# Low-rank attention on one core: row and key scores in 64-row pairs, with the PSUM banks shared out anew

## The chip, the cores and the metric

One core of a Trainium2 chip runs the whole program. The metric is the device time of one execution in microseconds. The kernel before took 1809.59 us (median of three runs, 1809.46 to 1812.57). Engines are TensorE (PE, with its weight loads as PEld), VectorE (DVE), ScalarE (ACT), GpSimd (POOL) and SyncE (SP), which issues the DMAs.

## The reference

The reference is a network of five residual steps on x of 8 x 1024 x 128: a gated low-rank layer, attention in windows, the gated layer again, a quantised layer, and at last attention over low-rank projections. The change is in the last, which is cut here to what matters (8 batches, s = 1024, 8 heads, d_k = 128, d_c = d_hr = 32):

```python
c_q, c_kv = h_t @ W_DQ + b_DQ, h_t @ W_DKV + b_DKV            # 32 wide
q_c, k_c, v_c = (c_q @ W_UQ + b_UQ), (c_kv @ W_UK + b_UK), (c_kv @ W_UV + b_UV)   # split into 8 heads of 128
q_r = (c_q @ W_QR + b_QR)                                     # 8 heads of 32
k_r = h_t @ W_KR + b_KR                                       # 32, the same for all heads
scores = concat(q_c, q_r) @ concat(k_c, k_r).T / sqrt(160)
o = softmax(scores) @ v_c
x = x + o @ W_O + b_O
```

## The kernel before, in words

The program is one sequence per engine, with semaphores between them. Stages follow each other: window attention until about 500 us, the quantised layer, and from about 585 us to the end the low-rank attention, which also carries the rest of the next batch's norm and the last quantised layer ("extra items").

**The arithmetic.** The key weights are multiplied into the query weights once, so that scores are products of 64 numbers (32 of c_kv, 32 rotary) on either side. To keep precision with fp32r matmuls, both sides are split into a high and a low part. A key tensor `key_hl` holds high parts in partitions 0 to 63 and low parts in 64 to 127; `q_hi` holds the query's high part twice, `q_low` the low part and a row of shifts. A head (one of 64, numbered u) has eight steps g, each with a tile of 128 keys or query rows.

**Steps.** The code goes through steps g with an order per engine written by a planner, `low_rank_plan`. In a step PE does, for each half of 512 columns, a *row score* (line 1825, for the head whose scores come 14 steps later, `ROW_LEAD`) and the *key scores* (lines 1878 and 1882, two matmuls that accumulate). VectorE takes the maximum of each row score (line 1833) and every four steps collects them (line 1841); GpSimd makes the shifts (lines 1853, 1857) and SyncE moves them into the last row of `q_low` (line 1864), 4 DMAs for each half of a head. ScalarE takes the exponential of each half (line 1893) into `prob`, a ring of 8 tiles. GpSimd adds seven of the eight tiles of a head with six additions (lines 1904 and 1907).

At every fourth step PE weighs the values with four tiles of `prob` (line 1936), and at step 3 of 8 it also forms the totals of the head before from the added tiles and the eighth (line 1929). VectorE inverts the totals (line 1946) and multiplies (line 1953); SyncE moves the head's result away.

**Queries.** Two query items per head (line 1641, four steps apart) go to bank 7; ScalarE copies each to `q_hi` (line 1702) one step later, VectorE makes `q_low` (line 1754) a step after that, before the maxima of that step.

**Banks.** PSUM has eight banks. Key scores have a ring of three (0 to 2), the weighed values bank 3, row scores and totals a ring of three (4 to 6) and all items bank 7 (the last batch spreads some). A use of a ring waits for what emptied the bank three uses before (`row_bank_free`), an item for what emptied the item before (`low_bank_free`, line 1495).

**Extra items** are started by the planner at even steps without a query: "turn" (line 1670), "low" (line 1674, then VectorE's lines 1765 and 1768), "const" (1680), "value" (1687), "proj" (1650, then 1760), "quant" (1657) and "product" (1664, then 1743), the last two and the "quantise" steps for the layer of the batch before. Norm statistics (line 485) and aggregation (line 493) come at VectorE's steps too. Between PE and the other engines there is no other order than these semaphores, so an engine that waits holds up all that is behind it.

## Time and profile before

| | |
|---|---|
| time, median of three runs | 1809.59 us |
| the profiled execution's span | 1812.5 us |
| PE busy (weight loads) | 1670.4 us, 92% (1223.0, 67%) |
| VectorE, ScalarE, GpSimd busy | 1393.8 (77%), 1137.5 (63%), 1177.3 (65%) |
| chain that ended last | PE 54%, VectorE 11%, GpSimd 2% |
| exponentials, line 1893 | 1024 x 597 ns |
| maxima, line 1833 | 1024 x 682 ns |
| additions, lines 1904 and 1907 | 2.4 us each |

Busy times are unions over an engine's instructions. Matmuls overlap each other and the ends of their records are modelled, so on PE the distance between the starts of two matmuls says what one costs. In the chain the profile names, for each stretch, the engine whose work was waited for.

### The profile page before, as it was taken

Reading aid. Unit: us, or ns where it says so; the run is one execution under the profiler, and the core shown is the slowest. Engines: PE = TensorE matmul, PEld = TensorE weight load, DVE = VectorE, ACT = ScalarE, POOL = GpSimd, SP = SyncE. Lnnn points to the kernel's source line nnn. Section 1 sums busy time; section 2 is a strip of 40 time slices with the busy share of each in tenths; the row PEclk is TensorE's granted clock in tenths of the full one; section 3 lists DMA queues with packets and bytes.
Section 4 is the critical chain, followed back from the end, with each engine's and each line's share of the span. In section 5 each row is a group of like instructions: output and inputs, shape, how many; then the busy total and the mean of one; then the engine's idle time right before and its main releaser. Section 6 shows DMA issues by size and latency. Waiting matters only on the chain.

```text
span 1812.5 us, 39662 instructions
## 1 busy us (share of the span) xinstructions
PE 1670.4 (92%) x15057; PEld 1223.0 (67%) x15057; DVE 1393.8 (77%) x2976; ACT 1137.5 (63%) x2222; POOL 1177.3 (65%) x909
## 2 busy tenths in 40 slices
PE   4679999999877899999999999999999999999995
PEld 4557777777766567666766766766676677677674
DVE  5557777766597888878888888888887888888862
ACT  5447777777676466666666666666656666665662
POOL 4300111000066498898898988989889898898892
PEclk9889999999887899999999999999999999999997
DMA  4556666654000000000000000001001000100101
GB/s 123 136 140 156 162 156 159 164 136 116 29 1 1 1 10 8 10 8 10 7 13 16 10 8 19 11 7 22 7 10 19 8 10 7 22 7 10 19 10 30
DMA packets 198677, 81.47 MB, mean 45 GB/s; under 512 B 152553, under 2 KB 177493, under 8 KB 198357
## 3 DMA queue, kind: packets, MB, share of 16 engines
q1 hardware_dynamic: 198484, 78.93, 19.5%
q8 instruction: 119, 1.95, 0.5%
q14 instruction: 74, 0.60, 0.1%
HBM read 39.79 MB, written 29.88 MB: 38 GB/s over the span
## 4 chain that ended last, share of the span: by engine, by line
PE 54%; DVE 11%; POOL 2%; issue 1%; ACT 1%; DMA 0%; SPq 0%; POOLq 0%; ACTq 0%
PE pair L1825 12%; PE pair L1878 11%; PE pair L1882 11%; PE pair L1936 10%; DVE amax L1833 4%; PE pair L1929 4%; PE pair L1650 2%; DVE o_inv L1946 1%; PE pair L1641 1%; DVE stats L485 1%; POOL w_mix L1907 1%; PE pair L1664 1%; DVE q_low L1754 1%; DVE cq L1765 1%; DVE key_hl L1768 1%
## 5 line engine op out<-in xcount | busy, mean ns | idle before, releaser
L1893 ACT ACTIVATE prob<-pair 128x512 f32<-128x512 f32 x1024 | 604.4, 597 | 422.2 <-PE pair L1882 359.6
L1833 DVE TENSOR_REDUCE amax<-pair 128x1 f32<-128x512 f32 x1024 | 670.3, 682 | 133.9 <-PE pair L1825 131.8
L1825 PE MATMUL pair<-key_hl,q_hi 128*128 128x512 f32 x1024 | 437.8, 430 | 11.2 <-DVE amax L1833 7.1
L1878 PE MATMUL pair<-q_hi,key_hl 128*128 128x512 f32 x1024 | 405.2, 396 | 2.6 <-ACT prob L1893 2.6
L1882 PE MATMUL pair<-q_low,key_h 65*128 65x512 f32 x1024 | 406.0, 396 | 0.0
L1907 POOL TENSOR_TENSOR w_mix<-w_mix,prob 128x1024 f32<-128x1024 f32 x160 | 382.3, 2389 | 25.2 <-ACT prob L1893 8.5
L1907 POOL TENSOR_TENSOR Wm<-Wm,prob 128x1024 f32<-128x1024 f32 x155 | 369.6, 2384 | 20.8 <-ACT prob L1893 4.1
L520 POOL TENSOR_SCALAR veps<-mv 128x8 f32<-128x8 f32 x47 | 11.4, 243 | 452.6 <-DVE mv L493 451.2
L1825 PEld LDWEIGHTS pair<-key_hl,q_hi 128*128 128x128 f32 x1024 | 196.1, 192 | 115.9 <-issue 51.0
L1936 PE MATMUL pair<-prob,values 128*32 128x256 f32 x4096 | 247.2, 382 | 0.0
L1186 DVE TENSOR_REDUCE mx_neg<-pair 128x4 f32<-128x512 f32 x256 | 164.9, 687 | 94.8 <-PE pair L1090 94.1
L1878 PEld LDWEIGHTS pair<-q_hi,key_hl 128*128 128x128 f32 x1024 | 195.5, 191 | 44.3 <-ACT prob L1893 9.4
L1882 PEld LDWEIGHTS pair<-q_low,key_h 65*128 65x128 f32 x1024 | 192.5, 188 | 44.6
L1936 PEld LDWEIGHTS pair<-prob,values 128*32 128x32 f32 x4096 | 127.5, 110 | 100.9 <-issue 25.0
L1136 ACT ACTIVATE yT<-pair 128x512 f32<-128x512 f32 x256 | 138.6, 593 | 72.3 <-PE pair L1042 70.3
L1946 DVE RECIPROCAL o_inv<-pair 128x256 f32<-128x256 f32 x64 | 112.5, 1758 | 59.8 <-PE pair L1929 59.8
L542 ACT ACTIVATE y<-x,mean_neg,rstd 128x128 f32<-128x128 f32 x336 | 137.7, 485 | 19.0 <-POOL mean_neg L528 18.9
L1090 PE MATMUL pair<-keys,queries 64*128 64x128 f32 x1024 | 100.5, 317 | 0.0
L1042 PE MATMUL pair<-queries,keys 64*128 64x128 f32 x1024 | 97.0, 309 | 0.0
L1702 ACT ACTIVATE q_hi<-pair 128x512 fp32r<-128x512 f32 x128 | 75.7, 591 | 20.0 <-PE pair L1641 20.0
L1754 DVE TENSOR_TENSOR q_low<-pair,q_hi 64x512 fp32r<-64x512 f32 x128 | 86.3, 675 | 2.2 <-ACT q_hi L1702 2.2
L1090 PEld LDWEIGHTS pair<-keys,queries 64*128 64x128 f32 x1024 | 82.7, 199 | 3.7
(209 smaller groups left out, 2232.8 us busy)
## 6 DMA issues: line engine op xcount, KB each, us to landing
rows_mem<-once SPq DMA_DIRECT2D x128, 128.0 KB, 2.0
queries<-rows_mem SPq DMA_DIRECT2D x64, 256.0 KB, 4.5
keys<-rows_mem SPq DMA_DIRECT2D x16, 1024.0 KB, 7.1
rows_mem<-once SPq DMA_DIRECT2D x128, 64.0 KB, 1.9
q_low<-shift_cols SPq DMA_DIRECT2D x512, 0.5 KB, 2.0
yT<-o_norm SPq DMA_DIRECT2D x256, 32.0 KB, 1.9
x<-x_dram SPq DMA_DIRECT2D x8, 512.0 KB, 7.3
out_dram<-x SPq DMA_DIRECT2D x7, 512.0 KB, 3.4
```

The costliest lines, as they stand in the source:

```text
L542: ins = e.activation(y_of(stage, b)[:, t, :], x[:, b * NT + t, :], ACT.Identity, bias=mean_neg[:, k, t:t + 1], scale=rstd[:, k, t:t + 1])
L1090: ins = e.matmul(bank(S_BANKS[r])[:, q * P:(q + 1) * P], queries[rows, hb % QUERY_BUFS, q, m].rearrange("p s w -> p (s w)"), keys[rows, b ...
L1136: e.activation(pT[:, u % P_TURNED].rearrange("p q k -> p (q k)"), key_row_bank(*divmod(u, 2)), ACT.Exp).then_inc(*exps.up(u))
L1186: e.tensor_reduce(mx_neg[:, hb % 2, r, :, m], bank(S_BANKS[r]).rearrange("p (q k) -> p q k", q=QUADS), AX_X, ALU.max, negate=True).then_in ...
L1825: e.matmul(row_bank(("row", r, i)), q_hi[:, k, t * P:(t + 1) * P], key_hl[:, b % 2, i * HALF:(i + 1) * HALF], start=True, stop=True, skip_ ...
L1833: e.tensor_reduce(amax1[:, u % 2, t, i:i + 1], row_bank(("row", r, i)), AX_X, ALU.max).then_inc(*row_maxed.up((r, i)))
L1878: e.matmul(bank(j), key_hl[:, b % 2, ks], q_hi[:, k, sl], start=True, stop=False, skip_group_check=True)
L1882: e.matmul(bank(j), key_h1[:, b % 2, ks], q_low[:, k, sl], start=False, stop=True, skip_group_check=True).then_inc(*key_scored.up((g, half)))
L1893: e.activation(prob1[:, g % P_BUFS, half * HALF:(half + 1) * HALF], bank(K_BANKS[(2 * g + half) % 3]), ACT.Exp, scale=SCALE1).then_inc(*ke ...
L1907: e.tensor_tensor(into, into, p, ALU.add).then_inc(*summed_keys.up(g))
L1936: ins = e.matmul(bank(PVB)[q * DC:(q + 1) * DC, 0:QUARTER], values[:, b % 2, t, :], prob1[:, g % P_BUFS, q * QUARTER:(q + 1) * QUARTER], s ...
L1946: e.reciprocal(o_inv[:, u % 2, :], row_bank(("total", u, 0))[:, 0:QUARTER]).then_inc(*o_inverse.up(u))
```

## The change

All of it is in the low-rank stage (and a few names beside it):

- **Row scores.** Keys are kept as `key_high` and `key_low`, each with the same 64 rows in partitions 0 to 63 and 64 to 127. Queries are kept as 128 x 512: the first 512 queries in the upper 64 partitions, the last 512 in the lower. A row step issues two matmuls of 64 rows, one for each side, on 128 queries of either side and 512 keys. Row scores use the high parts alone. Both sides' banks are waited for ahead of the first.
- **Key scores.** Four matmuls of 64 rows for each side of a tile (high x high, low x high, high x low, ones x shift), in two banks; a ring of two pairs of banks (0 to 3). Key scores come ahead of row scores in a step.
- **Exponentials.** One of 128 x 1024 over both banks of a tile.
- **Query.** One item per head, at step 7 of 8, two matmuls that accumulate in one bank; `q_low` is one operation of 128 x 512.
- **Banks.** Weighed values in bank 4; banks 5, 6, 7 are one ring for rows, queries, items and totals.
- **Items** start at step 3 of 8 only, up to two: one ahead of the totals (not "low") and one behind the weighing. Projections move from step 12 to 18 of a batch's 64, the quantise steps by 4.
- **Totals.** Five additions instead of six; the totals are formed from three parts. They are inverted straight from PSUM as before: the functions of another way (`spread_out`) stand in the code but `spread_out` is always False.
- **Shift.** One maximum over the head's eight tiles, one pair of shift operations, eight DMAs into a tensor of its own, `q_shift`.
- "low" has three operations on VectorE instead of two, "value" sixteen matmuls instead of eight.

```diff
-PIPELINE = 16
+PIPELINE = 17
+PVB, SHARED_BANKS = 4, (5, 6, 7)
+SUMMED = 6
...
+    def use(key):
+        places[key] = SHARED_BANKS[len(uses) % 3], uses[-3] if len(uses) >= 3 else None
+        uses.append(key)
+        return places[key]
...
+        u, rest = divmod(g + PIPELINE, NT)
+        return ("query", u, 0) if rest == 0 and 0 <= u < U else None
...
+        if 0 <= g + ROW_LEAD < NT * U:
+            for side in range(2):
+                use(("row", g + ROW_LEAD, side))
         item = regular(g)
-        if item is None and waiting and (g % 2 == 0 or g >= NT * U):
+        if item is None and waiting and (g >= NT * U or g % NT == 3 and waiting[0][0] != "low"):
             item = waiting.pop(0)
...
+        if g % NT == 3 and 0 <= g // NT - 1 < U:
+            use(("total", g // NT - 1, 0))
+        if g % NT == 3 and 0 <= g < NT * U and waiting and (item is None or waiting[0][0] != "low"):
+            run = begin(waiting.pop(0))
+            after.append((tuple(run[:3]), 1))
...
+        def pe_row_scores(e, r):
+
+            u, t, half = row_tiles(r)
             b, k = u // NH, u % Q_BUFS
-            e.wait_ge(*q_hi_done.at((u, t // 4)))
+            e.wait_ge(*q_hi_done.at((u, 0)))
...
+            for side in range(2):
+                shared_bank_free(e, ("row", r, side))
+            for side in range(2):
+                rows = slice(side * KR, (side + 1) * KR)
+                e.matmul(shared_bank(("row", r, side)), q_hi[rows, k, t * P:(t + 1) * P],
+                         key_high[rows, b % 2, half * HALF:(half + 1) * HALF], start=True, stop=True,
+                         skip_group_check=True).then_inc(*row_scored.up((r, side)))
...
+            if g >= 2:
+                e.wait_ge(*key_exp.at(g - 2))
+            for part in range(4):
...
+                for side in range(2):
+                    rows = slice(side * KR, (side + 1) * KR)
+                    weights = ones_shift[rows, :] if part == 3 else (key_low if part == 1 else key_high)[rows, b % 2, ks]
+                    moving = (q_hi, q_hi, q_low, q_shift)[part][rows, k, :]
+                    ins = e.matmul(banks[side], weights, moving, start=part == 0, stop=part == 3, skip_group_check=True)
...
+            e.activation(prob1[:, g % P_BUFS, :], pair[g % 2][:, :], ACT.Exp, scale=SCALE1).then_inc(*key_exp.up(g))
...
-                    e.wait_ge(*summed_keys.at(NT * u + 6))
-                    parts = prob1[:, (NT * u + 7) % P_BUFS, :], key_sum[u % 2]
+                    e.wait_ge(*summed_keys.at(NT * u + SUMMED - 1))
+                    parts = *(prob1[:, (NT * u + t) % P_BUFS, :] for t in range(SUMMED, NT)), key_sum[u % 2]
...
-                for half in range(2):
-                    if 0 <= g + ROW_LEAD < total:
-                        pe_row_scores(e, g + ROW_LEAD, half)
-                    if 0 <= g < total:
-                        pe_key_scores(e, g, half)
+                if 0 <= g < total:
+                    pe_key_scores(e, g)
+                if 0 <= g + ROW_LEAD < total:
+                    pe_row_scores(e, g + ROW_LEAD)
```

## Rows read from the trace of the kernel before

**Rows 1.** The page's part 1: busy time, share, instructions.

```profile
PE 1670.4 (92%) x15057; PEld 1223.0 (67%) x15057; DVE 1393.8 (77%) x2976; ACT 1137.5 (63%) x2222; POOL 1177.3 (65%) x909
```

**Rows 2.** Line 1946's inversions: all, and two eight heads apart (timeline: start, duration).

```profile
L1946 DVE RECIPROCAL o_inv<-pair x64: 1757/1758/1759, 635.5 to 1783.7; 128x256 f32<-128x256 f32 x64
...
775.76 1.76 DVE L1946 RECIPROCAL o_inv<-pair 128x256 f32<-128x256 f32 x1 [0.80 <-PE pair L1929]
...
924.53 1.76 DVE L1946 RECIPROCAL o_inv<-pair 128x256 f32<-128x256 f32 x1 [0.80 <-PE pair L1929]
```

**Rows 3.** Groups: count, busy us, mean ns, idle before and its releaser.

```profile
L1893 ACT ACTIVATE prob<-pair 128x512 f32<-128x512 f32 x1024 | 604.4, 597 | 422.2 <-PE pair L1882 359.6
...
L1254 ACT ACTIVATE d_q<-yT,cst 128x1024 fp8e4<-128x1024 f32 x7 | 8.0, 1141 | 0.0
...
L1254 ACT ACTIVATE d_q<-yT,cst 128x512 fp8e4<-128x512 f32 x2 | 1.4, 722 | 1.7 <-POOL yT L1247 1.7
```

**Rows 4.** Timeline of VectorE in a head without extra items.

```profile
690.73 1.76 DVE L1946 RECIPROCAL o_inv<-pair 128x256 f32<-128x256 f32 x1 [0.43 <-PE pair L1929]
...
707.37 1.76 DVE L1946 RECIPROCAL o_inv<-pair 128x256 f32<-128x256 f32 x1 [0.43 <-PE pair L1929]
```

**Rows 5.** Timeline of PE in the same head.

```profile
692.89 0.39 PE L1882 MATMUL pair<-q_low,key_h 65*128 65x512 f32 x1
693.12 0.40 PE L1825 MATMUL pair<-key_hl,q_hi 128*128 128x512 f32 x1
...
698.02 0.40 PE L1882 MATMUL pair<-q_low,key_h 65*128 65x512 f32 x1
698.35 1.93 PE L1936 MATMUL pair<-prob,values 128*32 128x256 f32 x32
700.22 0.50 PE L1825 MATMUL pair<-key_hl,q_hi 128*128 128x512 f32 x1
...
706.24 0.64 PE L1929 MATMUL pair<-prob,ones_col 128*32 128x256 f32 x8
706.69 0.61 PE L1929 MATMUL pair<-w_mix,ones_col 128*32 128x256 f32 x8
```

**Rows 6.** Timeline, all engines, around a start and around a release.

```profile
1040.61 0.39 PE L1825 MATMUL pair<-key_hl,q_hi 128*128 128x512 f32 x1
...
1041.04 0.69 DVE L1833 TENSOR_REDUCE amax<-pair 128x1 f32<-128x512 f32 x1 [0.24 <-PE pair L1825]
...
1051.65 0.63 DVE L493 BATCH_NORM_AGGREGATE mv<-stats 128x2 f32<-128x6 f32 x8
...
1052.78 1.27 DVE L1833 TENSOR_REDUCE amax<-pair 128x1 f32<-128x512 f32 x2
...
1053.51 0.19 PEld L1825 LDWEIGHTS pair<-key_hl,q_hi 128*128 128x128 f32 x1 [0.90 <-DVE amax L1833]
...
1053.84 0.39 PE L1878 MATMUL pair<-q_hi,key_hl 128*128 128x512 f32 x1
```

**Rows 7.** Timeline of PE in the window stage: matmuls of 64 rows in pairs.

```profile
401.31 0.39 PE L1085 MATMUL pair<-mask_bf,both_rows 64*128 64x512 bf16 x2 [0.17 <-DVE mx_neg L1186]
401.35 0.74 PE L1090 MATMUL pair<-keys,queries 64*128 64x128 f32 x8
401.93 0.39 PE L1035 MATMUL pair<-both_rows,mask_bf 64*128 64x512 bf16 x2
```

**Rows 8.** Timelines: shift DMAs, statistics, a projection, one operation of a low product.

```profile
833.40 1.24 SPq L1864 DMA_DIRECT2D q_low<-shift_cols  x2
...
1046.30 0.86 DVE L485 BATCH_NORM_STATS2 stats<-x 128x6 f32<-128x128 f32 x4
...
781.89 1.95 PE L1650 MATMUL pair<-w_out,yT 128*128 128x128 f32 x16
783.60 0.48 PE L1825 MATMUL pair<-key_hl,q_hi 128*128 128x512 f32 x1
...
827.42 0.75 DVE L1765 SCALAR_TENSOR_TENSOR cq<-pair,Wt,cq 32x512 fp32r<-32x512 f32 x1
```

More of the change, by code:

```diff
@@ L251, in regular @@
     def regular(g):
-        for i in range(2):
-            u, rest = divmod(g + 16 - 4 * i, NT)
-            if rest == 0 and 0 <= u < U:
-                return "query", u, i
-        return None
-    opening = {"bias": [((("bias", 0, 0), None, None), 1)]}
+        u, rest = divmod(g + PIPELINE, NT)
+        return ("query", u, 0) if rest == 0 and 0 <= u < U else None
+    opening, had = {"bias": [((("bias", 0, 0), None, None), 1)]}, {}
     for item, j in zip(prepare(0), (2, 3, 4, 5, 2, 3)):
-        run = begin(item, j)
-        opening.setdefault(item[0], []).extend((tuple(run[:3]), part) for part in range(1, PARTS[item[0]] + 1))
+        opening.setdefault(item[0], []).extend(((item, j, had.get(j)), part) for part in range(1, PARTS[item[0]] + 1))
+        had[j] = item
     steps, running, waiting = [], [], []
@@ L1636, in pe_low_part @@
                 return
-            low_bank_free(e, before)
+            if item not in places_m or before:
+                low_bank_free(e, before)
             if kind == "query":
@@ L1683, in pe_low_part @@
             else:
-                e.wait_ge(*mla_built.at("both"))
+                e.wait_ge(*mla_built.at("first dims"))
                 e.wait_ge(*keys_done.at((a, 1)))
+                e.wait_ge(*key_copied.at((a, 1)))
                 for t in range(NT):
-                    ins = e.matmul(bank(j)[:, t * DC:(t + 1) * DC], key_hl[:, a % 2, t * P:(t + 1) * P], both_parts[:, :],
-                                   start=True, stop=True, skip_group_check=True)
+                    for part in (key_high, key_low):
+                        ins = e.matmul(bank(j)[:, t * DC:(t + 1) * DC], part[:, a % 2, t * P:(t + 1) * P],
+                                       first_dims[:, :], start=part is key_high, stop=part is key_low,
+                                       skip_group_check=True)
                 ins.then_inc(*value_done.up(a))
@@ new lines, in pool_shift @@
+        def pool_shift(e, u):
+            b, h = divmod(u, NH)
+            top, mc = (shift[:, n, :] for n in range(2))
+            c = ccol[:, b % 2, :, h]
+            e.wait_ge(*row_topped.at(u))
+            e.wait_ge(*const_ready.at(b))
+            if u:
+                e.wait_ge(*shift_steps.at((u - 1, 2)))
+            e.tensor_tensor(mc, top, c, ALU.add).then_inc(*shift_steps.up((u, 1)))
+            e.wait_ge(*shift_steps.at((u, 1)))
+            if u:
+                e.wait_ge(*shift_ready(u - 1))
+            e.tensor_tensor(shift_cols[:, :], c, mc, ALU.subtract).then_inc(*shift_steps.up((u, 2)))
@@ new lines, in sync_move_shift @@
+        def sync_move_shift(e, u):
+            e.wait_ge(*shift_steps.at((u, 2)))
+            queries_free(e, u)
+            if u == 0:
+                e.wait_ge(*set_low.at("shift rows"))
+            for t in range(NT):
+                side, n = divmod(t, NT // 2)
+                e.dma_start(q_shift[side * KR:side * KR + 1, u % Q_BUFS, n * P:(n + 1) * P].bitcast(F32).rearrange(
+                    "o (p t) -> o p t", t=1), shift_cols[:, t:t + 1].bitcast(F32)).then_inc(
+                    shift_moved[u % Q_BUFS], 16)
@@ L1822, in pe_row_scores, with pe_key_scores @@
+        def pe_key_scores(e, g):
+            u, t = divmod(g, NT)
+            b, k = u // NH, u % Q_BUFS
+            ks = slice(t * P, (t + 1) * P)
+            banks = [bank(g % 2 * 2 + side) for side in range(2)]
             if u % NH == t == 0:
                 e.wait_ge(*keys_done.at((b, 1)))
-            row_bank_free(e, ("row", r, i))
-            e.matmul(row_bank(("row", r, i)), q_hi[:, k, t * P:(t + 1) * P], key_hl[:, b % 2, i * HALF:(i + 1) * HALF],
-                     start=True, stop=True, skip_group_check=True).then_inc(*row_scored.up((r, i)))
@@ L1896, in pool_sum @@
+        def act_exponentials(e, g):
+            if g >= P_BUFS:
+                before = g - P_BUFS
+                e.wait_ge(*pv_done.at(before // 4))
+                if before % NT < SUMMED:
+                    e.wait_ge(*summed_keys.at(max(before % NT, 1) + before // NT * NT))
+            for side in range(2):
+                e.wait_ge(*key_scored.at((g, side)))
+            e.activation(prob1[:, g % P_BUFS, :], pair[g % 2][:, :], ACT.Exp, scale=SCALE1).then_inc(*key_exp.up(g))
         def pool_sum(e, g):
@@ L2013, in pe_low_rank @@
                     pe_weigh(e, g // 4 - 1)
+                for (item, j, before), part in after:
+                    pe_low_part(e, item, j, before, part)
         def act_low_rank(e):
-            for g, early, late in plan_m:
+            for g, early, late, after in plan_m:
                 if g == LAST_C["copy"]:
@@ L2056, in dve_low_rank @@
         def dve_low_rank(e):
-            for g, early, late in plan_m:
+            for g, early, late, after in plan_m:
                 if g == CONST_AT + 1:
```

300 lines of the change are left out of this document (157 added, 143 removed).

## The prediction, before the result was known

> **What bounds the kernel now.** I read the page first. TensorE is busy 92% of the span and no other engine over 77% [rows 1]; but the ends of its records are modelled, so I went on to the views by time. The changed part runs from about 585 us to the end, 64 heads one after another. Eight heads take 924.53 - 775.76 = 148.8 us [rows 2], 18.6 us each, and all others the same but for the first and last eight; the list of groups gives durations [rows 3]; the timelines of PE and VectorE over one head show what binds.
>
> A head with nothing but its own work takes 707.37 - 690.73 = 16.64 us between two inversions [rows 4]. On PE the starts of 512-column matmuls are 0.234 us apart (692.89 to 693.12; 0.234 as a mean over many), also where the rows differ (128 or 65): one slot [rows 5]. Going from scores to weighing adds 0.10 (698.02 to 698.35). One part of the totals, and likewise one tile weighed, costs 0.44 (706.24 to 706.69, less the 0.01 of a first group); four are 1.76, and from 698.35 to 700.22 and the 0.10 of a bare load (below) are 1.97, so coming back costs 0.2. PE needs 50 slots x 0.234 = 11.7, weighing 3.5, totals 0.9, changes 0.6: 16.7 us. **PE is exactly the bound of a clean head**. The other 148.8 - 8 x 16.64 = 15.7 us of a batch are extra PE items (about 11: projections, turns, low-rank products) and some 4 of stalls.
>
> Those stalls are the key. The row scores go to PSUM banks that VectorE must empty by a maximum. A maximum begins 0.43 us after its matmul starts (1040.61 to 1041.04), lasts 0.69, and frees the bank; the next weight load starts 0.05 after that end (first of the two at 1052.78, mean 0.68, ends 1053.46; load 1053.51), and the load itself then lies bare: next start after 0.335 instead of 0.234, so 0.10 more [rows 6]. **Chain matmul, maximum, bank free, matmul: 0.43 + 0.69 + 0.15 = 1.28 us.** Before, a half row uses the bank of three half rows earlier, 3 x 0.70 = 2.10 us: slack 0.82. At 1053.5 VectorE had come from 1.13 us of other work (1051.65 to 1052.78), and PE, full before, idled there: the slack is what is used up first [rows 6].
>
> **The change part by part.**
>
> *Row scores in 64-row pairs*: 8 pair slots a head instead of 16, if the two sides run together. The window stage shows such pairs: two 512-column matmuls of 64 rows end within 0.39 us, the time of one, and 2 x 512 + 8 x 128 columns take 401.93 - 401.31 = 0.62 us [rows 7], where one after another they would need 4 x 0.234 = 0.94. So a pair costs one slot, and I take 0.234. Gain 8 x 0.234 = 1.87. *Key scores*: four pair slots a tile instead of four: nothing. *Query*: two matmuls as before. *Totals* from three parts instead of two: +0.44. Changes of mode: +0.1 (64 to 128 rows before the query). PE work of a clean head: 40 slots 9.4, query 0.47, weighing 3.5, totals 1.3, changes 0.7: **15.35 us**, 1.3 below before.
>
> *Banks.* Three banks now carry both sides of every row step, the query, the totals and every extra item. Row step g+1 takes the banks of (g-1, side 1) and (g, side 0): it must wait for the first maximum of the step right before it. A step of PE is 5 slots = 1.17, the chain is 1.28: slack is -0.11 where it was +0.82. And step 1 of each head takes the bank of the query, which is free only when VectorE has written q_low, queued behind both maxima of step 0. Going by the durations above (VectorE starts the next maximum 0.60 after the last when both are ready: 1.27 for two [rows 6]), with R for the start of a row step, R0 = 0:
> step 0 maxima 0.43 and 1.03; q_low 1.63 to 2.30; R1 = 2.45 (PE alone: 1.17). Maxima 2.88, 3.48; R2 = 3.73. Small maximum 4.20; maxima 4.28, 4.88; R3 = 5.11. The totals take the bank of (2, side 1): 5.56 + 0.15 = 5.71. Totals to 7.0, weighing to 8.75, change 0.19, four slots: R4 = 9.87. Then three chains: R5 = 11.14, R6 = 12.42, R7 = 13.70. The query takes the bank of (6, side 1): 14.30; two slots, change, weighing, change, four slots: R0' = **17.7 us**. That is 1.07 more than 16.64 though PE works 1.3 less; PE idles 2.4.
>
> *Extra work in a batch* (the plan puts items only at step 3 of 8, one before the totals and one behind the weighing): projections 16 x 0.107 twice (781.89 to 783.60) [rows 8] = 3.8 with changes; by the same 0.11 a matmul turns 8, const and value 24, transposes 8, products 16, with 0.1 to 0.3 for each change or bank: 1.2, 2.9, 1.2, 2.0. The two low products are dear: 0.9 + 0.1 on PE (fp32, taken as twice the 0.47 of two slots; 0.47 is the lower bound), and then VectorE does three operations of 0.75 at step 5 instead of two, 2.3 in a row [rows 8], ahead of the row maxima, while row step 5 waits for their bank: +2.8 each, together 7.6. Statistics (0.86 with its end, 0.8) and aggregation (0.63) at steps 1 and 2 [rows 6, 8], twice a batch, and one reduction of 0.6 lie bare in the chain: 3.5. At steps 0 and 4 the weighing hides them. Sum 22.2. A full batch: 8 x 17.7 + 22.2 = 163.8, against 148.8: **+15.0**.
>
> *Exponentials of 128x1024*: 0.60 for 512 columns, and line 1254 takes 0.42 more for 1024 than for 512 columns (1.141, 0.722): 1.02; above that 1.14 (all of line 1254) and 1.19 (two of 0.60) [rows 3]. Key step g+2 needs exponential g: 0.43 + 1.02 + 0.15 = 1.60 from its last matmul, and comes after 1.28 + 0.47 = 1.75. At 1.14 it still fits, at 1.19 it would cost 0.02 a step. Nothing. *Five additions*: GpSimd loses one of six a head; with 65% [rows 1] it isn't the bound, so nothing; only in the last two heads, where no row scores are left, may its chain count: 0 to -5, taken as -3. *Shift*: one group of eight DMAs behind one maximum instead of two of four; issues are 0.6 apart [rows 8], so 5 us, and a few to land, ready near 12 of the 16.8 us there are, under the row and key scores between. Cover 5 us; with it gone the loss would be the excess. *q_low* of 128x512 once for 64x512 twice: -0.6 on VectorE, inside the above.
>
> **Sum.** Six full batches 6 x 15.0 = 90; the first has fewer items (8 x 17.7 + 13.2 = 154.8, against 775.76 - 635.5 = 140.3 [rows 2]): +14.5; the last +5 after the 3 won at its end; start of the pipeline (rows only, chain 1.28 against 1.20) +4. Together +113.5 on the span of 1812.5: 1926. The median shown is 1809.6, 0.16% below the profiled span, so **1923 us**.
>
> A page and a row: the trace shows two row tiles at once, with a change from one mode to another of 0.1. The Trainium skill, TensorEngine Tiling (Array Packing), PSUM Bottleneck, says that tiling speeds up TensorE but not the emptying of PSUM, which may become the limit; "Mode switching requires drain" stands there too. It speaks against this change and agrees with the chain; no number above hangs on it.
>
> **Rivals.** (1) *PE stays the bound; faster.* If the bank chain didn't bite (a release so quick that it comes under 5 slots, 1.17 us, and q_low not in the way), a batch would be 8 x 15.35 + 12.5 items + 4.5 stalls = 139.8, -9.0; over 7.75 batches -70: 1740. For it: in the trace of before such waits cost little. Against: the chain is 1.28 by three measured terms, and q_low is in VectorE's order. It decides at a chain of 1.17 us. (2) *Loads in row mode aren't hidden*: each slot 0.10 more. 40 slots are 4.0 a head, of which 1.6 fills PE's idle: 64 x 2.4 = 154 on top: 2077. Against: 401.31 to 401.93 leaves no room for five bare loads. The Trainium skill, TensorE: Matmul & The Clock Gate, Part 3, says loads overlap only with matmuls in other row groups; that is this rival, and the rows so far speak against it. (3) *The pairs don't run together with 512 fp32r columns*: 80 slots, 24.7 us a head: 64 x 7 = 450 more: 2370. Shown are only 128-column pairs of fp32r and 512-column ones of bf16. (4) *Both effects cancel*: within 0.2%; needs the chain at about 1.2 and q_low at half its price.
>
> **Chances.** Forecast 0.80, (1) 0.11, (2) 0.04, (3) 0.02, (4) 0.03. The forecast's own range is 1870 to 1975: 7 us for each 0.02 in the chain's five steps, 30 for the items, 25 for a slot between 0.22 and 0.255 (the chain hides part). The range 1860 to 1985 leaves out the rivals. A measurement here can tell 0.2% from no change. Faster 0.12, same 0.03, slower 0.85.
>
> **What would show it.** Row matmul starts 1.28 apart in steps 4 to 7 and 2.4 between steps 0 and 1; PE idle some 2.4 us a head, released by the maxima and by q_low; heads of 17.7 at the start and 163 to 165 for a batch; PE busy share down, VectorE's about equal. Wrong if row starts come at 1.17, if the pairs' starts are far apart, or if releases come in 0.05 without the bare load.

## The result and the profile after

| | before | after |
|---|---|---|
| device time, median | 1809.5 us (1805.7 to 1812.6, 4 runs) | 1966.7 us (1962.9 to 1972.2, 4 runs) |
| profiled span | 1812.5 us | 1964.5 us |
| first to last inversion | 1148.2 us | 1290.5 us |

The change makes the kernel slower: the ratio is 1.086, 95% interval 1.084 to 1.089. The forecast was 1923, in a range from 1860 to 1985. The sign and the mechanism were right, and the loss was larger: 152 us on the span instead of 113.5.

The page's part 1 of the kernel after, which answers to [rows 1] (busy us, share, instructions):

```profile
PE 1707.6 (87%) x17673; PEld 1187.2 (60%) x17673; DVE 1348.1 (69%) x2865; ACT 1047.4 (53%) x1646; POOL 1004.0 (51%) x719
```

Every engine has a smaller share than before, and none has taken PE's place. That is how it looks when a chain through several engines has become the bound. TensorE has 37 us more in its records, though the change takes eight slots from a head; where these come from is shown below (bare loads, and matmuls at half the clock).

The loop alone, from the first inversion to the last, before and after (columns: us, busy time and instructions of PE, PEld, DVE, ACT, POOL, then the granted clock, DMA share, GB/s):

```profile
635.49:1783.73 1148.24, 1129.00 (x8773) 787.09 (x8769) 937.59 (x1647) 719.38 (x1301) 1016.63 (x698) 1.00 0.08 12
```

```profile
643.77:1934.30 1290.53, 1166.27 (x11324) 754.42 (x11320) 891.36 (x1539) 631.95 (x740) 844.99 (x511) 0.97 0.07 10
```

PE stood idle for 19 us of the loop before and for 124 us of it after. Who it waited for in that stretch, by the view of waits (engine, line, releaser: us in total, times, longest us); L1858 is the row matmul, L1783 q_low, L1798 key_low, L1867 the maxima:

```profile
PE pair L1858 <- DVE q_low L1783: 73.0, 60, 1.8
...
PE pair L1858 <- DVE key_low L1798: 38.7, 14, 2.8
...
PE pair L1858 <- DVE amax L1867: 7.0, 13, 0.6
```

These three make 119 of the 124 us. All are waits of a row matmul for one of the three shared banks. Before, no line of PE's waits in the loop has more than 5.7 us.

The inversions [rows 2], now of line 1984, and two of them eight heads apart:

```profile
L1984 DVE RECIPROCAL o_inv<-pair x64: 1755/1758/1760, 643.8 to 1934.3; 128x256 f32<-128x256 f32 x64
```

```profile
803.16 1.76 DVE L1984 RECIPROCAL o_inv<-pair 128x256 f32<-128x256 f32 x1 [1.11 <-PE pair L1967]
...
971.90 1.76 DVE L1984 RECIPROCAL o_inv<-pair 128x256 f32<-128x256 f32 x1 [1.11 <-PE pair L1967]
```

A batch takes 168.7 us, where it took 148.8. A head with nothing but its own work is one with 17.95 us between inversions (728.92 to 746.87). PE in such a head, from the query on (start, us, engine, line, operation; in brackets the idle time ahead and its releaser):

```profile
736.01 0.51 PE L1665 MATMUL pair<-cq,w_query 98*128 98x512 f32 x1
...
739.57 0.39 PE L1858 MATMUL pair<-key_high,q_hi 64*128 64x512 f32 x2
739.80 0.40 PE L1920 MATMUL pair<-q_hi,key_high 64*128 64x512 f32 x2
740.03 0.39 PE L1920 MATMUL pair<-q_hi,key_low 64*128 64x512 f32 x2
...
741.94 0.50 PE L1858 MATMUL pair<-key_high,q_hi 64*128 64x512 f32 x2 [1.05 <-DVE q_low L1783]
...
743.31 0.50 PE L1858 MATMUL pair<-key_high,q_hi 64*128 64x512 f32 x2
...
744.71 0.49 PE L1858 MATMUL pair<-key_high,q_hi 64*128 64x512 f32 x2
```

Each row is a pair (x2) of 64-row matmuls, and the next pair starts 0.23 us later: a pair is one slot. From step 0 (739.57) to step 1 (741.94) it is 2.37 us, with PE idle for 1.05 of them until q_low is written. The next steps are 1.37 and 1.40 apart, where five slots would be 1.17.

The groups that answer to [rows 3] and the maxima (busy us, mean ns, then the idle time before and its releaser):

```profile
L1867 DVE TENSOR_REDUCE amax<-pair 128x1 f32<-128x512 f32 x1024 | 658.6, 685 | 311.8 <-PE pair L1858 300.8
L1932 ACT ACTIVATE prob<-pair 128x1024 f32<-128x1024 f32 x512 | 523.3, 1024 | 556.0 <-PE pair L1920 496.3
```

The 128x1024 exponential takes 1.02 us, as estimated, and ACT waits for PE.

### The profile page after: what moved, and what is told of

Read it like the earlier page. It is cut to its first block, busy times and chain, and to the rows that moved or that the text cites. A ratio compares the mean times of both kernels' runs of the same rounds, so it can differ in the third digit from the quotient of the medians.

```text
span 1964.5 us, 44406 instructions
## 1 busy us (share of the span) xinstructions
PE 1707.6 (87%) x17673; PEld 1187.2 (60%) x17673; DVE 1348.1 (69%) x2865; ACT 1047.4 (53%) x1646; POOL 1004.0 (51%) x719
## 4 chain that ended last, share of the span: by engine, by line
PE 65%; DVE 13%; SPq 6%; ACT 5%; issue 4%; DMA 4%; POOL 3%; POOLq 0%; ACTq 0%; DVEq 0%
PE pair L1920 21%; PE pair L1974 12%; PE pair L1858 10%; DVE amax L1867 5%; PE pair L1967 5%; DMA keys<-rows_mem 3%; DVE q_low L1783 2%; ACT y L556 2%; PE pair L1676 2%; PE pair L1665 2%; SPq L966 2%; SPq L946 2%; SPq L947 1%; PE pair L1075 1%; DVE key_low L1798 1%
## 5 line engine op out<-in xcount | busy, mean ns | idle before, releaser
L1867 DVE TENSOR_REDUCE amax<-pair 128x1 f32<-128x512 f32 x1024 | 658.6, 685 | 311.8 <-PE pair L1858 300.8
L1932 ACT ACTIVATE prob<-pair 128x1024 f32<-128x1024 f32 x512 | 523.3, 1024 | 556.0 <-PE pair L1920 496.3
L1858 PE MATMUL pair<-key_high,q_hi 64*128 64x512 f32 x1024 | 252.6, 480 | 132.9 <-DVE q_low L1783 78.2
L1945 POOL TENSOR_TENSOR w_mix<-w_mix,prob 128x1024 f32<-128x1024 f32 x128 | 304.8, 2381 | 38.5 <-ACT prob L1932 22.4
L1858 PEld LDWEIGHTS pair<-key_high,q_hi 64*128 64x128 f32 x1024 | 109.9, 194 | 274.4 <-DVE q_low L1783 106.0
L1920 PE MATMUL pair<-q_hi,key_high 64*128 64x512 f32 x1024 | 227.7, 431 | 0.9 <-ACT prob L1932 0.9
L1920 PE MATMUL pair<-q_shift,ones_shift 64*128 64x512 f32 x1024 | 215.3, 406 | 0.5 <-DMA q_shift<-shift_cols 0.5
L1920 PE MATMUL pair<-q_low,key_high 64*128 64x512 f32 x1024 | 214.3, 404 | 0.0
L1920 PE MATMUL pair<-q_hi,key_low 64*128 64x512 f32 x1024 | 212.8, 401 | 0.0
L1920 PEld LDWEIGHTS pair<-q_shift,ones_shift 64*128 64x128 f32 x1024 | 105.6, 192 | 18.8 <-DMA q_shift<-shift_cols 0.9
L1920 PEld LDWEIGHTS pair<-q_low,key_high 64*128 64x128 f32 x1024 | 105.4, 192 | 18.8
L1920 PEld LDWEIGHTS pair<-q_hi,key_low 64*128 64x128 f32 x1024 | 105.9, 193 | 11.6
```

The source lines that it names most:

```text
L1858: e.matmul(shared_bank(("row", r, side)), q_hi[rows, k, t * P:(t + 1) * P], key_high[rows, b % 2, half * HALF:(half + 1) * HALF], start=Tr ...
L1867: e.tensor_reduce(amax1[:, u % 2, NT // 2 * side + t, half:half + 1], shared_bank(("row", r, side)), AX_X, ALU.max).then_inc(*row_maxed.up ...
L1920: ins = e.matmul(banks[side], weights, moving, start=part == 0, stop=part == 3, skip_group_check=True)
L1932: e.activation(prob1[:, g % P_BUFS, :], pair[g % 2][:, :], ACT.Exp, scale=SCALE1).then_inc(*key_exp.up(g))
L1945: e.tensor_tensor(into, into, p, ALU.add).then_inc(*summed_keys.up(g))
```

## The experiments

All times are medians; the kernel before stood beside each run, at 1808.7 to 1813.8 us. "The loop" is the time from the first to the last inversion; it leaves out the start, which differs by up to 12 us between kernels with the same work up to there. It comes from one trace of each kernel, and the executions of one kernel differ by 2 to 13 us, so a difference of two loops of a few us is only a rough figure. Where stretches at half the clock are counted, one of double length counts as two.

**q_low ahead of the maxima.** The query item is one step shorter, so that VectorE writes q_low in step 0 before that step's two maxima:

```diff
-    PARTS = {"query": 3, ...
+    PARTS = {"query": 2, ...
-            elif kind == "query" and part == 3:
+            elif kind == "query" and part == 2:
```

> The changed kernel, with q_low made one step earlier: at step 0 of 8, ahead of that step's maxima, while PE weighs. Bank-chain theory: the bank of the query is free long before row step 1, so that step comes 1.34 us after row step 0 instead of 2.46: 1.1 a head, 64 x 1.1 = 70, about 1895 us, clean heads of 16.8 instead of 17.95. Rival, that VectorE is short of time as a whole: it does the same work, so no change (1966). Rival, that PE's slots in 64-row mode or its changes of mode are the loss: no change (1966).

Measured: 1889.2 us, 77.5 less than the changed kernel. The waits for q_low are gone; those for key_low stand as they were:

```profile
PE pair L1858 <- DVE key_low L1798: 38.7, 14, 2.8
...
PE pair L1858 <- DVE amax L1867: 15.7, 33, 0.5
```

A clean head takes 16.81 us instead of 17.95. So the order of one VectorE operation is worth half of what the change loses.

**One wait instead of two.** Where both banks of a row step were last read by maxima, PE waits for the later one alone (the second maximum always starts behind the first in VectorE's timeline, so its end covers the other):

```diff
-            for side in range(2):
-                shared_bank_free(e, ("row", r, side))
+            if any(not places_m[("row", r, side)][1] or places_m[("row", r, side)][1][0] != "row"
+                   for side in range(2)):
+                shared_bank_free(e, ("row", r, 0))
+            shared_bank_free(e, ("row", r, 1))
```

> The changed kernel; where both banks of a row step were last used by row scores, PE waits for the later of the two maxima alone, which implies the earlier, instead of for both one after the other. The step chain came out at 1.34 us where 1.28 was forecast, and the load starts 0.115 instead of 0.053 after the maximum's end. If the second wait is the cause: 0.06 in 4 to 5 steps a head, 64 x 0.27 = 17, about 1949 us, row starts 1.28 apart. If the 0.06 belongs to the 64-row pairs themselves (their matmuls or their loads): no change (1966).

Measured: 1956.0 us, 10.7 less; in the loop it is 6.1 (1284.4 us against 1290.5), and the clean head only shrinks from 17.95 to 17.88. The release itself did what was expected. In the changed kernel the load starts 0.115 us after the maximum's end (the maximum of 716.713 ends at 717.403, the load of line 1858 starts at 717.518), and with one wait it is 0.053, the number of [rows 6]. But the gain of the step is smaller. PE with one wait in steps 1 to 3:

```profile
726.59 0.50 PE L1859 MATMUL pair<-key_high,q_hi 64*128 64x512 f32 x2
...
727.84 0.50 PE L1859 MATMUL pair<-key_high,q_hi 64*128 64x512 f32 x2
...
729.12 0.51 PE L1859 MATMUL pair<-key_high,q_hi 64*128 64x512 f32 x2
```

The steps are 1.25 and 1.28 instead of 1.34 us, and no shorter, since VectorE then has its maxima back to back: in the run with both edits four of them take 2.57 us, 1.285 for the two of a step.

```profile
721.50 2.57 DVE L1868 TENSOR_REDUCE amax<-pair 128x1 f32<-128x512 f32 x4
```

And part of what the steps win is given back where the totals and the query wait for the same maxima. With R for the start of a row step and R0' for step 0 of the next head, R3 to R4 is 4.88 instead of 4.80, R7 to R0' 4.16 instead of 4.07. The expected size was wrong; the chain was not.

**A longer maximum.** VectorE reads 256 columns of the bank once more ahead of the first maximum of each step:

```diff
+            if side == 0:
+                e.tensor_reduce(spare[:, 0:1], shared_bank(("row", r, side))[:, 0:QUARTER], AX_X, ALU.max)
```

> The changed kernel with one more maximum on VectorE at each row step, over 256 of the columns, ahead of the first maximum, its result unused (the output is unchanged). About 0.33 us each. Bank-chain theory: it is added to the chain in steps 1, 2, 3, 5, 6, 7, and to the wait for q_low: 2.0 to 2.3 a head, 130 to 150 us, about 2105. Rival, PE's own work is the bound and VectorE (busy 69%) has time: 2.6 us a head fit into its idle time: at most 20 us, about 1980.

Measured: 2100.3 us, 133.6 more: 0.26 us for each of 512 operations of 0.42 (0.34 to the start of the maximum behind it). VectorE is busy for only 69% of the span, and three quarters of the 0.34 us still come through.

**More PE work.** The first key pair of every tile is issued twice, one slot of 0.234 more in each step:

```diff
-            for part in range(4):
+            for part in (0, 0, 1, 2, 3):
```

> The changed kernel with the first pair of key matmuls of each tile issued twice, the second overwriting the first (the output is unchanged): one more slot of 0.234 a step on PE, outside the chain of row banks. Bank-chain theory: PE waits at row steps 1, 2, 5, 6, 7, so the slot lies in the wait there (0.07 left of it in four steps, nothing in step 1) and costs in full only where PE comes from weighing: 0.8 a head, about 50 us, 2017. Rival, PE's work is the bound: 8 x 0.234 = 1.87 a head, 120 us, 2086.

Measured: 2002.9 us, 36.2 more, where 512 x 0.234 = 120 were added and about 50 expected. So PE, busy for 87% of the span, passes on 30% of what is added, and VectorE with 69% passes on 75%. The granted clock is in both numbers: the loop has 28 stretches at half the clock with the longer maximum and 13 with the added slot, where the changed kernel has 20. At 1.15 us each (see below), the two loops (130.4 us longer and 37.7 longer) would give some 70% and 38% without it. The order stays. Which engine is in the chain is told by these two runs, and not by the shares. The steps are no longer 1.34 but 1.40 apart (739.42, 740.82, 742.21), which is six slots: the slack was the difference.

**Both early steps together.**

> Both of the earlier steps together: q_low at the first step ahead of the maxima, and one wait in place of two where both banks were last read by maxima. Nothing is left out. If the bank chain is the bound and the two savings lie at different links of it, they add up: 1966.7 - 77.5 - 10.7 = 1878, a clean head at 17.95 - 1.13 - 0.36 = 16.5, which is below the PE bound of the kernel before (16.65). Rival (PE is the bound again as soon as the chain is short, so that the second saving is lost in clean heads): 1885 and more, clean head 16.8.

Measured: 1881.3 us; the clean head takes 16.75 us, PE's records cover 16.46 of them. The loop is 1207.7, 12.4 less than with q_low alone. The time lies between the theory's 1878 and the rival's 1885, and the clean head is that of the rival: it gained 0.06 us, 3.8 in 64 heads, and most of the rest of the 12.4 are 7 stretches at half the clock fewer in the loop, 8 instead of 15 (below). By the medians of the whole kernel the second edit is worth 7.9 us on top of the first.

**The low products.** What the forecast did not have is seen in PE's timeline of the changed kernel behind a low product:

```profile
849.59 0.40 PE L1920 MATMUL pair<-q_low,key_high 64*128 64x512 f32 x2
849.82 0.40 PE L1920 MATMUL pair<-q_shift,ones_shift 64*128 64x512 f32 x2
852.98 0.50 PE L1858 MATMUL pair<-key_high,q_hi 64*128 64x512 f32 x2 [2.76 <-DVE key_low L1798]
853.33 0.40 PE L1920 MATMUL pair<-q_hi,key_high 64*128 64x512 f32 x2
...
855.35 0.66 PE L1920 MATMUL pair<-q_hi,key_low 64*128 64x512 f32 x2
855.78 0.66 PE L1920 MATMUL pair<-q_low,key_high 64*128 64x512 f32 x2
856.21 0.66 PE L1920 MATMUL pair<-q_shift,ones_shift 64*128 64x512 f32 x2
856.63 0.66 PE L1858 MATMUL pair<-key_high,q_hi 64*128 64x512 f32 x2
```

PE stands still for 2.76 us, as the forecast says (2.8). Then, about 1 us after it has started again, the slots are 0.43 us apart: the granted clock is 0.5, the 1.2 GHz level, for a short stretch. It is back at 1.00 by 857.6, and the next pairs of that view, from 860.18 on, are 0.23 apart again. The loop of the kernel before has one such stretch, at its very end; the loop of the changed kernel has 20, of which 13 begin around the end of a wait for key_low and 7 elsewhere. Two intervals of the changed kernel with the same work and the same waits (2.8 for key_low, 1.1 for q_low, 0.6 for a maximum) give the price:

```profile
1351.18:1374.73 23.55, 19.05 (x180) 12.05 (x176) 16.41 (x25) 13.51 (x20) 14.60 (x12) 0.93 0.06 8
1519.84:1542.29 22.45, 17.94 (x180) 10.98 (x176) 16.42 (x25) 13.38 (x20) 14.61 (x12) 1.00 0.06 8
```

One stretch costs 1.10 us here, and 1.1 to 1.26 in other such pairs; below I take 1.15. That the clock fell in one and not in the other, behind equal waits, also says that a single wait does not settle it.

*Taken ahead of the totals.* The low products begin in the same step, but in front of the totals, and their VectorE part comes one step earlier:

```diff
-    PARTS = {..., "low": 4, ...
+    PARTS = {..., "low": 3, ...
-        if item is None and waiting and (g >= NT * U or g % NT == 3 and waiting[0][0] != "low"):
+        if item is None and waiting and (g >= NT * U or g % NT == 3):
-        if g % NT == 3 and ... and waiting and (item is None or waiting[0][0] != "low"):
+        if g % NT == 3 and ... and waiting and waiting[0][0] != "low" and (item is None or item[0] != "low"):
-            elif kind == "low" and part == 3:        (VectorE; ACT's copy from 4 to 3)
+            elif kind == "low" and part == 2:
```

> The changed kernel with one thing moved: the two low products of a batch take their bank ahead of the totals' bank and not behind it, and the DVE and ACT parts of a low product come one step earlier. Nothing is left out. Theory (a low product costs its wait, and then a stretch at the 1.2 GHz level): in the changed kernel the second row pair behind a low product waits 2.76 us for key_low (R4 to R5 4.09 us and not 1.34), and some 3.4 us behind it the granted clock is 0.5, which costs 1.15 us (intervals of 23.83 and 23.89 against 22.71 with and without it, in the run with q_low early). Taken ahead of the totals, the same DVE work lies inside the 4.2 us from the totals to R4, which PE waits through anyhow. 14 low products x 2.75 = 38 us for the wait alone, 14 x 1.15 = 16 more if the clock stays up: 1967 - 54 = 1913, in a range from 1905 to 1935, with 14 waits on L1798's line nearly gone and fewer than 12 stretches at 0.5 between 640 and 1940 us (20 before). Theory without the clock: 1929, stretches as before. Rival (the wait goes to the next use of the same DVE time, since the row pair R4 then stands behind the low product): no gain, 1960 to 1970.

Measured: 1954.8 us, 12.0 less instead of 54. PE still waits 31.3 us for key_low (38.7 before this edit), and VectorE's timeline, with one row of PE, says why:

```profile
843.53 1.76 DVE L1984 RECIPROCAL o_inv<-pair 128x256 f32<-128x256 f32 x1 [1.23 <-PE pair L1967]
...
845.32 0.75 DVE L1794 SCALAR_TENSOR_TENSOR cq<-pair,Wt,cq 32x512 fp32r<-32x512 f32 x1
...
846.10 1.50 DVE L1798 SCALAR_TENSOR_TENSOR key_low<-pair,Wt,key_high 64x512 fp32r<-64x512 f32 x2
...
847.75 0.51 PE L1858 MATMUL pair<-key_high,q_hi 64*128 64x512 f32 x2 [1.44 <-DVE key_low L1798]
```

The low product is there at 842.0 and ACT's two reads of it end at 843.5, but VectorE takes it only behind the inversion, which waits for the totals, which now stand behind the low product on PE. I had counted the 4.2 us of PE work as cover, and not what VectorE has in its queue in that time. This holds for 8 of the 14 low products, which now cost a wait of 1.4 us. For the second one of batches 2 to 7 the wait is 3.3 us, longer than before the edit, since two operations of the quantised layer stand in VectorE's queue as well:

```profile
866.59 1.61 DVE L1557 TENSOR_SCALAR d_scale<-d_amax 128x32 f32<-128x32 f32 x1
868.23 0.35 DVE L1560 RECIPROCAL d_rscale<-d_scale 128x32 f32<-128x32 f32 x1
...
871.05 0.56 PE L1858 MATMUL pair<-key_high,q_hi 64*128 64x512 f32 x2 [3.34 <-DVE key_low L1798]
```

The loop is 13.5 us shorter (1277.1). The waits for key_low are 7.4 of it, and there were 12 stretches at half the clock instead of 20, which at 1.15 each would be 9 more; the two together are over what was gained, so how it divides is not shown.

*A shorter read.* The second of key_low's subtractions is left out for batches 2 to 7:

```diff
-                for rows in (slice(0, KR), slice(KR, P)):
+                for rows in (slice(0, KR), slice(KR, P))[:2 if a < 2 else 1]:
```

> The changed kernel with the second of the two subtractions that fill key_low (rows 64 to 127) left out for batches 2 to 7, so that what is computed for those batches lacks that part; batch 1 keeps it and stands in the same trace as the control. The wait of the row pair behind a low product becomes some 0.7 us shorter (2.76 to about 2.05). Theory of the wait alone: 12 x 0.72 = 8.6 us less, 1958. Theory with the clock depending on how long PE has stood still: if 2.05 us no longer brings the clock down, 12 x 1.15 = 14 us more is saved, 1944, and the stretches at 0.5 between 640 and 1940 us fall from 20 to some 8; if it does, 1958 with the 20 stretches. Rival (the low product's cost is ACT's or PE's): 1966, and the wait stays at 2.76.

Measured: 1955.4 us, 11.3 less; the loop is 1276.3, 14.2 less, of which the waits for key_low (29.5 us instead of 38.7) are 9.2 and three stretches at half the clock (17 instead of 20) 3.5. The wait is 2.0 us now, while batch 1, which keeps both subtractions, still waits 2.8; the low clock still comes, only less often. Two intervals with the same waits:

```profile
1015.52:1037.21 21.69, 17.97 (x180) 10.90 (x176) 15.66 (x24) 13.40 (x20) 14.65 (x12) 1.00 0.06 8
1180.75:1203.70 22.95, 19.23 (x180) 11.80 (x176) 15.67 (x24) 13.51 (x20) 14.23 (x12) 0.93 0.05 7
```

Of the 12 intervals with a low product in batches 2 to 7, 7 have the longer time, where the changed kernel has 11. Neither expectation on the clock holds: it is neither all nor none.

*A longer read.* VectorE reads the low product's bank once more:

```diff
+                if a >= 2:
+                    e.tensor_reduce(spare[:, 0:1], bank(j), AX_X, ALU.max)
                 for rows in (slice(0, KR), slice(KR, P)):
```

> The opposite of e8_low_short: in the changed kernel, DVE reads the low product's bank once more for batches 2 to 7 (a maximum over 512 columns, 0.69 us, whose result is not used), ahead of the two subtractions of key_low. Nothing is left out. The wait of PE behind a low product becomes some 0.7 us longer, 2.76 to 3.45. By the wait: 12 x 0.69 = 8.3 more, 1975. The clock: the price of some 1.15 us shows in 11 of the 12 low products of batches 2 to 7 of the changed kernel already, so at most 1.2 us more: 1976, with 12 of 12. If the fall of the clock had nothing to do with how long PE stands still there, the number of intervals with that price would be free to go either way; in e8_low_short it was 7 of 12.

Measured: 1973.6 us, 6.9 more; the waits for key_low are 47.2 us instead of 38.7, 12 x 0.71. In the loop it is 13.4 more (1303.9), of which 8.5 are the wait, one more stretch at half the clock 1.2, and some 4 are not accounted for; the profiled execution took 6.3 us more than the median of the four. All 12 intervals have a stretch at half the clock, one of them two. So over three lengths of the same wait, 2.0, 2.8 and 3.5 us, 7, 11 and 12 of 12 intervals lose clock. This alone doesn't show that the length decides: with the wait left at 2.8 us it was 12 of 12 with q_low early, 8 with one wait, and 8 with both edits. The ends are clearer: in the kernel with the low products ahead of the totals none of the 8 waits of 1.4 us was followed by a fall of the clock, and all 6 of 3.3 were.

**All of it, and statistics moved.** On top of both early steps, the low products ahead of the totals, and VectorE's statistics and aggregation in steps 0 and 4 of a head and not in 1 and 2, its quantisation steps likewise:

```diff
+            for n in {0: (1, 2), 4: (3,), 6: (7,), 7: (8,)}.get(r, ()):
+                early.append(((("norm", b + 1, n), None, None), 1))
-    QUANTISE = dict(zip((24, 25, 26, 28, 30, 31, 32, 33, 34, 35, 36, 37, 40, 45, 52), range(15)))
+    QUANTISE = tuple(zip((24, 24, 28, 28, 30, 31, 32, 33, 36, 36, 40, 41, 43, 48, 54), range(15)))
```

> The two steps of the run before, the low products ahead of the totals, and DVE's statistics and quantisation moved from the steps in which the chain sets the time to steps 0 and 4 of a head, where PE waits for other things. Nothing is left out. From 1878: low products 14 x 2.75 to 3.9 = 38 to 54 less, statistics and aggregation (3.5 us of bare DVE time in each of 7 batches, in the chain) 24 less: 1800 to 1816, forecast 1808, which is the time of the kernel before. The exchange of 50 slots of 0.234 for a chain of the same length then is worth nothing either way. Rival (the moved DVE work only delays the maxima of steps 0 and 4, which are in the chain as well): 1835 to 1850.

Measured: 1857.4 us. The loop has shrunk by 27.8 against both early steps (1179.9 against 1207.7), where 70 were expected; the low products' wait is 29.8 us, for the reason just shown, and that alone is most of what is missing. The time is above the range of the rival too (1835 to 1850). Of the 27.8, the shorter waits for key_low are 8.9 and two stretches at half the clock fewer 2; the 17 that are left stand against the 24 expected of the statistics.

**The second half of key_low copied by ACT.**

```diff
-                for rows in (slice(0, KR), slice(KR, P)):
+                for rows in (slice(0, KR),):
...
+                e.wait_ge(*keys_done.at((a, i)))
+                e.activation(key_low[KR:P, a % 2, sl], key_low[0:KR, a % 2, sl].bitcast(F32), ACT.Copy)
```

> The kernel of e5_all, with rows 64 to 127 of key_low filled by an ACT copy of rows 0 to 63 and not by a second DVE subtraction that reads the low product's bank: DVE has one operation of 0.74 us less in each of 14 low products, and leaves the bank that much earlier. Nothing is left out. The wait of 2.1 us behind a low product becomes 1.4, 14 x 0.74 = 10 us, and where the granted clock then stays up behind a low product, 1.15 us more each (7 of 14 intervals of e5_all show it): 1857 - 10 = 1847 by the wait alone, 1839 with the clock. Rival (ACT's extra copy is late and key_copied becomes the wait): 1857. By none of them is it under the 1812 of the kernel before.

Measured: 1851.5 us. The wait fell to 19.2 us, and the loop by 14.0 to 1165.8, with 3 stretches at half the clock instead of 6; its first inversion came 2.5 later, which the time of the run has in it. The loop of this kernel:

```profile
650.34:1816.18 1165.84, 1130.31 (x11324) 737.15 (x11320) 882.36 (x1526) 640.41 (x754) 844.36 (x510) 1.00 0.08 12
```

PE's records cover 1130.3 us, where the kernel before has 1129.0. That doesn't mean that 42 slots need as much of PE as 50 did. A record of a matmul behind a short wait has the bare load in it, and the modelled ends of those before it cover the wait. Take the starts in the clean head of the run with both edits (16.75 us). Six of its row steps come 1.25 to 1.34 apart instead of 1.17, which makes 0.7 in all. The two longer ones, with the totals and with the query, take 4.88 and 4.16, where the forecast's prices of PE's own work give 4.55 and 3.80: 0.7 more. Together this is the 1.4 us by which the head is above the forecast's 15.35 for PE alone. The loads lie bare only at pairs that wait for a maximum, and not at the two (719.73, 727.69) whose banks were free long before. So the clean head is still set by the maxima, mostly in waits too short for the view of waits.

No version tried beats the kernel before. The last one is 42 us behind it by the medians, 34 by the profiled spans, and of these 34 only 17.6 lie in the loop; the first inversion comes 14.9 us later than before, which no run looked into.

## Why the prediction was right, and where it was short

**The bound before and PE's slots: right.** Pairs start 0.23 us apart, 1024 columns in the time of 512. Rivals (2) and (3) are out by the same rows: loads are hidden inside a step, and bare only at a row pair that has waited and where the tile shape changes. Rivals (1), faster, and (4), no change, are out by the time.

**The bank chain: right, with one term too small.** The recurrence of a clean head against the trace, R being the start of a row step:

| from to | forecast | measured |
|---|---|---|
| R0 to R1, q_low behind two maxima | 2.45 | 2.37 |
| R1 to R2, R2 to R3 | 1.28, 1.38 | 1.37, 1.40 |
| R3 to R4, totals and weighing | 4.76 | 4.80 |
| R4 to R5, to R6, to R7 | 1.27, 1.28, 1.28 | 1.26, 1.35, 1.34 |
| R7 to the next R0, query and weighing | 4.0 | 4.07 |
| head | 17.7 | 17.95 |

The term was "bank free to matmul, 0.15" with a start of the maximum 0.43 behind the matmul. Of the steady step, 1.337 measured, the maximum has 0.69, the release up to the second load 0.147 (the forecast took 0.05 from [rows 6] and 0.10 for the load), and matmul to maximum 0.50, since the matmul's record there begins only 0.03 behind the start of its load, with the load inside it. Together the release is 0.06 longer: two waits stand ahead of the pair, and the run with one wait brought 0.115 back to 0.053. The head is 0.25 us longer than forecast, 2.0 a batch. The release is only part of that: without the second wait the steps come as forecast, but the head still takes 17.88, since the totals and the query then come later (4.88 and 4.16, forecast 4.76 and 4.0). These two are terms that the forecast had too small, and by more than it seemed before the wait was gone.

**PE's own work: right in the sum, but not a floor that could be reached.** The forecast has 15.35 us for a clean head and rival (1) a batch of 139.8. With q_low out of the way the head is 16.75, since a row pair that has to wait, however shortly, has its load bare (0.10) and VectorE needs 1.285 for the two maxima of a step, more than five slots. Rival (1) was further away than the 0.11 that it got.

**Extra work in a batch: right in the sum, its parts mostly not tested.** 22.2 us were forecast. The six full batches, 803.2 to 1812.7 us, take 168.3 each as a mean; less 8 x 17.95 that is 24.7, of which 17 stretches at half the clock in six batches, 1.15 each, are 3.3: 21.4 are left. The low products cost 2.8 us of wait each, as written (R4 to R5 4.09 and not 1.26). The other items were not measured one by one.

**The clock: not in the forecast.** It is the term that was missing. In the loop of the kernel before, PE's waits are 1.0 us at the longest but for a single one of 1.8, and the granted clock is 1.00; I took it as given for the kernel after as well, while I had myself put 2.4 us of idle PE into every head and 2.8 behind every low product. 20 stretches x 1.15 = 23 us, half of the 44 by which the forecast was short.

**First and last batch, and the edges.** The first batch lost 19.1 (forecast 14.5), with three of the 20 stretches in it, the last 4.3 (5). The first inversion came 8.3 us later, and the last one is 1.4 further from the end: 9.7, where the forecast has 4. At the start only row scores run, at half the clock: one step takes 1.64 us (606.95, 608.58, 610.22), with PE idle for 0.84 of it:

```profile
606.95 0.79 PE L1858 MATMUL pair<-key_high,q_hi 64*128 64x512 f32 x2 [0.87 <-DVE amax L1867]
608.58 0.80 PE L1858 MATMUL pair<-key_high,q_hi 64*128 64x512 f32 x2 [0.84 <-DVE amax L1867]
610.22 0.80 PE L1858 MATMUL pair<-key_high,q_hi 64*128 64x512 f32 x2 [0.84 <-DVE amax L1867]
```

The start was not tried by itself; since it varies between kernels that are alike up to there (638.8 to 650.3 for the first inversion), its 8.3 us are not all the change's.

**The difference put together.** Six full batches 26.8 (12 by the clean head's 0.25, 20 by the clock, -5 by the other extras, which is what is left over and hides errors of both signs), 2.0 since the seventh batch before took 146.9 and not 148.8, the first batch 4.6, the last -0.7, the edges 5.7: 38.4 of the 38.5 us between the forecast span of 1926 and 1964.5.

**The loss of the loop by cause**, each from the difference of two loops, in the order in which the edits were added: q_low behind the maxima 70.5 us; the second wait 12.4; statistics and the low products' place 27.8; key_low's second read 14.0; what is left 17.6. Together 142.3. The clock is in each of them (20, 15, 8, 6 and 3 stretches). Another order would share it out otherwise: the second wait is worth 6.1 when it is taken away first. By the medians of the whole kernel the same four steps are 77.5, 7.9, 23.8 and 6.0 us, with 42 left; only the first and third are well clear of the differences between executions in either account.

**Exponentials, additions, shift: right.** ACT waits for PE and not the reverse; PE waits for exponentials 0.9 us of the 124 and in the loop never for the shift's DMAs (once for 0.48 us ahead of it, at 635.4).

The Trainium skill, TensorEngine Tiling (Array Packing), PSUM Bottleneck, says that packing doesn't speed up the emptying of PSUM. The trace agrees: the packed matmuls ran two at a time in 0.23 us, and a maximum, which empties a bank, took 0.685 us as against 0.682 before. What the pairs would be worth with the banks of before is not shown: every run has pairs and three shared banks together.

## What to carry to other kernels

Before matmuls are packed, write down the loop from matmul to reader to free bank with the banks that will be left, and compare it with the matmuls of one step: here 1.34 us against 1.17, where spare banks had hidden it. In that loop look for the one operation of another kind whose bank is in the rotation (q_low, half of the loss): its place in the reader's queue matters more than its length. A share of busy time doesn't tell which engine is in the loop, but adding a known amount of work to each does: 75% came through from an engine busy for 69%, 30% from one busy for 87% (some 70 and 38 with the clock taken out). A look at the starts of the matmuls is needed beside the view of waits, since waits of 0.1 us don't stand in it. Before an operation is moved in one engine's order, look at what then stands ahead of it in the next engine's: that is where the low products lost what they were to gain. When a change puts idle time on TensorE, price the clock too.

## What the runs showed of the hardware that was not expected

- The granted clock fell to the 1.2 GHz level in a stage that had run at 2.4 but for one stretch at its end, around waits of 1.8 to 3.5 us in otherwise full work: in 7, 11 and 12 of 12 intervals for waits of 2.0, 2.8 and 3.5, but in 8 or 12 of 12 for the same 2.8 in other kernels; in 3 of 6 for 1.8 in the last kernel, in none of 8 for 1.4 and all of 6 for 3.3 with the low products ahead. Each fall costs 1.1 to 1.26 us, and 7 of the changed kernel's 20 stand at no such wait. It also came and stayed away behind equal waits, and its number fell from 15 to 8 by an edit that left those waits alone (2.8 us both times) and took 0.06 us from a step. What decides it is open.
- A second wait ahead of a matmul pair costs 0.06 us even when it is met: the load starts 0.115 instead of 0.053 us after the release.
- Two 64-row matmuls of 512 columns start 0 to 69 ns apart (median 4) and take the slot of one, 0.23 us, with the loads of the next pair hidden.
